# Heads dealt over both row halves, shifted products ahead of the scores, one maximum a round: an attention and expert kernel on one core

## What is computed

```
q, k, v    = split(layernorm(x) @ Wqkv + bqkv)          # 16 heads of 8
_, ka, va  = split(ctx @ Wqkv_aux + bqkv_aux)
p  = softmax(q k^T / sqrt(8));  pa = softmax(q ka^T / sqrt(8))
att = (1 - sigmoid(g)) * (p @ v) + sigmoid(g) * (pa @ va)
x  = x + tanh(g_xattn) * (att @ Wo + bo)
x  = x + tanh(g_ffn) * moe(layernorm(x))                 # 64 experts, top 8 of 4 of 8 groups, and a shared one
```

## Time and profile before

| | |
|---|---|
| runs | 859.24, 859.26, 859.61 us; median 859.26 |
| the profiled execution | 859.58 us, of which 857.8 us span |
| granted TensorE clock | 0.985 in the mean; half speed from 15.9 to 39.8 us, full after |
| busy | TensorE 826.2 us (96%), its weight loads 646.0, VectorE 683.6 (80%), ScalarE 566.8 (66%), GpSimd 637.3 (74%) |
| attention loop | from 36.4 us to about 288 us, 32 batches |

### The profile page before, as it was taken

One profiled execution on the slowest core, in us unless ns is written; L12 is line 12 of the kernel. 1 busy time (PEld: TensorE's weight loads), 2 busy tenths in 40 slices (PEclk: granted clock), 3 DMA queues, 4 the chain that ended last, 5 costly groups with the idle time before them and its releaser, 6 DMA issues.

```text
span 857.8 us, 20206 instructions
## 1 busy us (share of the span) xinstructions
PE 826.2 (96%) x6733; PEld 646.0 (75%) x6733; DVE 683.6 (80%) x1648; ACT 566.8 (66%) x964; POOL 637.3 (74%) x602
## 2 busy tenths in 40 slices
PE   4899999999999999999999999999999999999997
PEld 3477777777766678888888888878888888888885
DVE  6789999999897769769678877867966977876665
ACT  4388888888878665575576576557557557655554
POOL 2668888888854378877787786777777788778785
PEclk8599999999999999999999999999999999999999
DMA  4677786776652167447456554654654755546562
GB/s 119 173 169 173 178 183 155 187 169 170 160 126 51 53 152 169 120 111 184 117 142 147 131 142 125 154 135 109 163 139 111 171 130 134 149 116 150 137 138 58
DMA packets 108036, 120.04 MB, mean 140 GB/s; under 512 B 28560, under 2 KB 70352, under 8 KB 106496
## 3 DMA queue, kind: packets, MB, share of 16 engines
q1 hardware_dynamic: 105056, 118.23, 57.5%
q10 hardware_dynamic: 2880, 0.59, 0.4%
HBM read 103.55 MB, written 14.71 MB: 138 GB/s over the span
## 4 chain that ended last, share of the span: by engine, by line
PE 87%; DVE 5%; DMA 3%; issue 2%; SPq 1%; ACT 1%; POOL 0%; DVEq 0%; POOLq 0%
PE bank L1999 20%; PE bank L2000 20%; PE bank L2001 20%; PE bank L1336 7%; PE bank L1323 5%; PE bank L1294 3%; PE bank L1276 2%; PE bank L1344 2%; PE bank L1260 1%; PE bank L1357 1%; DVE mx L989 1%; PE bank L1270 1%; DMA cwb<-wts_scratch 1%; DMA stack_q<-nmaxT 1%; PE bank L1976 1%
## 5 line engine op out<-in xcount | busy, mean ns | idle before, releaser
L1676 POOL TENSOR_TENSOR hid<-act,cwb 128x512 f32<-128x512 f32 x264 | 424.0, 1615 | 126.4 <-DVE act L1903 69.1
L1729 ACT ACTIVATE silu<-bank 128x512 f32<-128x512 f32 x256 | 152.9, 597 | 190.7 <-PE bank L2001 189.9
L1903 DVE TENSOR_TENSOR act<-silu,bank 128x512 f32<-128x512 f32 (+1 forms) x264 | 180.5, 684 | 119.5 <-ACT silu L1729 78.7
L1999 PE MATMUL bank<-xhi,weights_hi 128*128 128x512 f32 x520 | 206.6, 397 | 0.0
L1911 DVE TENSOR_TENSOR hlo<-hid,hhi 128x512 fp32r<-128x512 f32 x256 | 197.5, 772 | 8.5 <-ACT hhi L1735 8.3
L2001 PE MATMUL bank<-xlo,weights_hi 128*128 128x512 f32 x520 | 204.2, 393 | 0.0
L2000 PE MATMUL bank<-xhi,weights_lo 128*128 128x512 f32 x520 | 203.9, 392 | 0.0
L1735 ACT ACTIVATE hhi<-hid 128x512 fp32r<-128x512 f32 (+1 forms) x264 | 164.8, 625 | 15.7 <-POOL hid L1676 13.1
L989 DVE TENSOR_REDUCE mx<-bank 128x4 f32<-128x512 f32 x240 | 156.0, 683 | 16.6 <-PE bank L1294 14.8
L786 ACT ACTIVATE prob<-bank 128x1024 f32<-128x1024 f32 x128 | 131.2, 1025 | 48.6 <-PE bank L1323 46.5
L2001 PEld LDWEIGHTS bank<-xlo,weights_hi 128*128 128x128 f32 x520 | 97.6, 188 | 22.0
(11 more groups left out here) (238 smaller groups left out, 1022.1 us busy)
## 6 DMA issues: line engine op xcount, KB each, us to landing
cwb<-wts_scratch SPq DMA_DIRECT2D x174, 384.0 KB, 5.4
stack_k<-k_scratch SPq DMA_DIRECT2D x30, 256.0 KB, 4.3
k_scratch<-parts_k SPq DMA_DIRECT2D x15, 384.0 KB, 3.4
stack_q<-q_scratch SPq DMA_DIRECT2D x30, 128.0 KB, 2.9
stack_k<-k_scratch SPq DMA_DIRECT2D x30, 128.0 KB, 5.2
q_scratch<-parts_q SPq DMA_DIRECT2D x15, 192.0 KB, 2.7
xin<-in_x_dram SPq DMA_DIRECT2D x16, 128.0 KB, 3.0
cin<-in_ctx_dram SPq DMA_DIRECT2D x16, 128.0 KB, 3.1
```

The costliest lines, as they stand in the source:

```text
L1676: pool.tensor_tensor(h_buf[k][:], a_buf[k][:], cwb[slot][:, q % GP, :], ALU.mult).then_inc(h_ok, 1)
L1729: act.activation(s_buf[k % RS][:], g_bank[k % 2][:], ACT.Silu).then_inc(s_ok, 1)
L1903: nc.vector.tensor_tensor(a_buf[k % RS][at], s_buf[k % RS][at], u_bank[k % 3][at], ALU.mult).then_inc(a_ok, 1)
L1999: nc.tensor.matmul(bank, w[0], mh, start=first, stop=False)
```

## The change

Heads are dealt in turn over the two halves: head h goes to row `ROW_OF[h]`, which is half h % 2, place h // 2. For this the weights of Q and K and their biases are reordered so (4-level patterns in place of 3-level ones); V and the output keep their order. The biases come in as rows, ScalarE reorders them, TensorE turns them into columns by three products with a one, and ScalarE copies these to `bcol`. The scores of a unit are still of one half and one bank, but the two units of a round are of different halves (`S_ROW`). In a round all 8 shifted products come first, half 0 and half 1 in turn, each half in a bank of its own; then the 4 scores, also in turn. One maximum of 128x1024 covers both score banks. The scores of a round therefore wait for the maximum of the whole round before. Both halves of a stack are waited for ahead of round 0. `first_scores` changes likewise.

The diff, cut to its core:

```diff
-S_HEAD = (8, 10, 12, 14, 0, 2, 4, 6)
+S_ROW = (0, 8, 2, 10, 4, 12, 6, 14)
+ROW_OF = tuple(h % 2 * (H // 2) + h // 2 for h in range(H))
...
     def bias_loads(sp):
-        turned = lambda a: a.rearrange("(h d a) -> d h a", d=DH, a=1)
-        for i, b in enumerate((turned(v["bqkv"][0:P]), turned(v["bqkv"][P:2 * P]), turned(v["bqkv_aux"][P:2 * P]))):
-            sp.dma_start(bcol[:, i:i + 1], b, allow_slow_non_contiguous=True).then_inc(c_in, 16)
+        sp.dma_start(brow_in[:, 0:2 * P], one(v["bqkv"][0:2 * P])).then_inc(c_in, 16)
+        sp.dma_start(brow_in[:, 2 * P:3 * P], one(v["bqkv_aux"][P:2 * P])).then_inc(c_in, 16)
...
+        def by_row(to, w):
+            act.activation(to.rearrange("p (d f i) -> p d f i", d=DH, f=2),
+                           w.rearrange("p (i f d) -> p d f i", d=DH, f=2), ACT.Copy).then_inc(wqk_ok, 1)
...
+        act.wait_ge(c_in, 16 * 2)
+        for i in range(3):
+            act.activation(brow[:, i * P:(i + 1) * P].rearrange("a (d f i) -> a d f i", d=DH, f=2),
+                           brow_in[:, i * P:(i + 1) * P].rearrange("a (i f d) -> a d f i", d=DH, f=2),
+                           ACT.Copy).then_inc(b_row, 1)
...
         evac_t(0, 0)
+        act.wait_ge(b_mm, 1)
+        act.activation(bcol[:], st_bank[0][:, 0:3], ACT.Copy).then_inc(b_ev, 1)
         clear_stack_q(0).then_inc(stack_clear, 1)
         clear_stack_q(1).then_inc(stack_clear, 1)
-        act.wait_ge(c_in, 16 * 3)
+        act.wait_ge(b_ev, 1)
         copy_q(0)
...
-        def maxima(b, par, u):
-            wait(dve, s_mm, UNITS * b + u + 1)
-            if u == 0:
+        def maxima(b, r, banks=two_banks):
+            wait(dve, s_mm, UNITS * b + 2 * r + 2)
+            if r == 0:
                 wait(dve, nm_ok, b - 1)
...
+            h = S_ROW[2 * r]
+            nc.vector.tensor_reduce(mx[b % 2][:, :, h:h + 2].rearrange("p (f a) h -> p f h a", f=2),
+                                    banks[:].rearrange("p (f h a k) -> p f h a k", f=2, h=2, a=2),
                                     AXX, ALU.max).then_inc(mx_ok, 2)
...
-                    if two_more:
-                        maxima(b + 2, odd, u)
+                    if two_more and u % 2 == 0:
+                        maxima(b + 2, u // 2)
                     if u == (1 if late else 0) and one_more:
                         evac_nmax(b + 1)
...
-        def stack_there(b, u):
+        def stack_there(b):
             n, c, s = b // CH, b % CH, b // CH % NST
             if c == 0:
-                wait(pe, stk[S_HEAD[u] // HH][s], 64 * ((n - 1) // NST + 1 if s else n // NST))
-            if u == 0:
-                wait(pe, shift_zero, CH if n == NST else b - CH * NST + 1)
+                for half in (1, 0):
+                    wait(pe, stk[half][s], 64 * ((n - 1) // NST + 1 if s else n // NST))
+            wait(pe, shift_zero, CH if n == NST else b - CH * NST + 1)
...
-            a, h = u % 2, (u // 2) * HPU + j
+            a, h = u % 2, ROW_OF[(u // 2) * HPU + j]
...
-            ins = nc.tensor.matmul(st_bank[u % 2][:, j * P:(j + 1) * P], k_of(n)[at, h % HH, c, a, :],
+            at_p = (a * 2 + j // 2) * P
+            ins = nc.tensor.matmul(st_bank[j % 2][:, at_p:at_p + P], k_of(n)[at, h % HH, c, a, :],
                                    q_of(n)[at, h % HH, c, :], start=True, stop=True)
-            if j == HPU - 1:
+            if a == 1 and j >= 2:
                 ins.then_inc(st_mm, 1)
...
         transposes(0, 0)
+        turn_biases()
         pe.wait_ge(wqk_ok, 3)
...
-                    if two_more and r % 2 == 0:
-                        stack_there(b + 2, 2 * r)
-                    for u in (2 * r, 2 * r + 1):
-                        ahead = (b + 2, u) if two_more else None
-                        shifted(b, u, 0)
-                        if ahead:
-                            scores(*ahead, 0)
-                        shifted(b, u, 1)
-                        shifted(b, u, 2)
-                        if ahead:
-                            scores(*ahead, 1)
-                        shifted(b, u, 3)
+                    if two_more and r == 0:
+                        stack_there(b + 2)
+                    u0, u1 = 2 * r, 2 * r + 1
+                    for u in (u0, u1):
+                        for j in range(HPU):
+                            shifted(b, u, j)
+                    if two_more:
+                        for j in range(2):
+                            scores(b + 2, u0, j)
+                            scores(b + 2, u1, j)
```

More of the change, by code:

```diff
@@ L227, in attention @@
     prob = [m(f"prob{i}", [P, 2, HPU * P], F32) for i in range(RP)]
+    brow, brow_in = (prob[0][0:1, k, 0:3 * P] for k in range(2))
     mx = [m(f"mx{i}", [P, 4, HH], F32) for i in range(2)]
@@ L1192, in on_dve @@
         for r in range(ROUNDS):
-            first_maxima(0, r)
+            maxima(0, r, (wide, two_banks)[r % 2])
         minus_max(0, 0, 3)
@@ L1198, in on_dve @@
         for r in range(ROUNDS):
-            first_maxima(1, r)
+            maxima(1, r, (wide, two_banks)[r % 2])
             if r == 1:
@@ L1301, in first_scores @@
             wait(pe, mx_ok, 2 * (pair - 1))
-            for u in (2 * r, 2 * r + 1):
-                for j in range(2):
-                    h = S_HEAD[u] + j
-                    if j == 0 and u in (0, 4):
-                        wait(pe, stk0[h // HH][b], 64)
+            if r == 0:
+                for half in (1, 0):
+                    wait(pe, stk0[half][b], 64)
+            for j in range(2):
+                for u in (2 * r, 2 * r + 1):
+                    h = S_ROW[u] + j
                     at = slice(*SCORE_ROWS[h // HH])
@@ L1358, in out_proj, with turn_biases @@
             nc.tensor.matmul(o, attT[:, 1, :], wo[:, 1, :], start=False, stop=True).then_inc(wo_mm, 1)
+        def turn_biases():
+            pe.wait_ge(b_row, 3)
+            pe.wait_ge(kones_ok, 4)
+            for i in range(3):
+                ins = nc.tensor.matmul(st_bank[0][:, i:i + 1], brow[:, i * P:(i + 1) * P], ones[0:1, 0:1],
+                                       start=True, stop=True)
+            ins.then_inc(b_mm, 1)
         def turn_max(b):
```

26 lines of the change are left out of this document (8 added, 18 removed).

## The result

| | before | after |
|---|---|---|
| median of the runs | 859.26 us (858.38 to 859.90, 5 runs) | 872.80 us (870.98 to 872.95, 5 runs) |
| the profiled execution | 859.58 us, span 857.8 | 870.98 us, span 869.2 |
| first batch of the loop starts | 36.43 us | 38.74 us |
| a pair of batches that no DMA delays | 15.59 us | 16.43 us |

A forecast was written before the change was run, and what follows sets the result against it. TensorE's own work was taken to bound five rounds of eight, the exponential loop three. 859.58 + 10.1 + 2.0 + 1.0 - 1.4 - 1.0 = 870.3 us, median 870.0; own range 865 to 875, stated 862 to 878.

The forecast's parts named there:

- What bounds the kernel: Attention stage: of eight rounds a pair, five are TensorE's own work, three are closed by shifted products, exponential, shifted products.
- the three waits: TensorE's waits for the exponential in three rounds of a pair: 0.1 us each over the gap, 0.3 a pair, would go.
- Part 1: Shifted products first over both halves: exponential starts at about +0.47 us, 0.22 earlier; TensorE's work stays, three waits go.
- Part 2: One maximum a round: 1.29 us becomes 1.21 on VectorE, starting at +0.64; the single buffer by itself costs nothing.
- The rival "faster": If nmaxT's DMA issue holds back nothing, the three waits go: 855.0 us, up to 859; chance 0.11.
- Part 3: Round 0: nmaxT's copy behind the whole maximum delays DMA issue, copy of Q and exponential; +0.78 us a pair, +10.1 total.
- There is a copy of Q in 13 odd batches: Loop: the count of batches that pay the delay behind nmaxT's DMA; of 16, the last three chunks have none; +10.1 us.
- Part 4: Both stack halves awaited ahead of round 0: stage start +2.0 us (0.8 to 3), late loads in the loop +1.0.
- The term of the loop: Six late stack loads, 4.1 us together, mostly forgiven by longer pairs: 0.5 left, +1.0 us taken, bounds 0 and 5.
- Part 5: Ends of the stage: -1.4 us in the last two batches, -1.0 in the three before; bias loads nothing.
- slower by the single buffer: Rival: scores wait for the maximum in most rounds; +5, 875 us; chance 0.07.
- The biases: Bias loads as rows, copies and small products lie beside other work: nothing, bounds 0 and +0.5 us.

The follow-up runs named there:

- e9_mended: Changed kernel with nmaxT's DMA issued in round 1, the maximum's semaphore stepping by 1, and first stores ahead of first loads: 862.19 us, 1.0032 of before.
- e1_ship_later: Changed kernel with only the issue of nmaxT's DMA moved, behind the copy of Q and round 1's exponential: 863.9 us, 1.0047 of before.
- e7_inc_one: Changed kernel with the joined maximum adding 1 to its semaphore instead of 2, waits on it counting rounds: 870.67 us, 1.0130 of before.
- e11_two_ship: Changed kernel with two maxima of 128x512 a round again and nmaxT's DMA issued in round 1 of every batch: 863.68 us, 1.0050 of before.
- e3_wide_on_before: Kernel before with only the joined 128x1024 maximum over both score banks a round: 873.40 us, 1.0155 of before.
- e5_copy_behind: Kernel before with only round 0's copy to nmaxT moved, behind both half maxima instead of between them: 866.49 us, 1.0072 of before.
- e4_both_halves: Kernel before with only the waits for both halves of a stack put ahead of round 0, first scores included: 863.13 us, 1.0043 of before.
- e6_bias_rows: Kernel before with only the new bias loads (two rows, three ScalarE copies, three products, one copy out): 860.91 us, 1.0010 of before.
- e10_wait_behind: Changed kernel, nmaxT's DMA in round 1, semaphore step 1, old store order, stack wait moved behind round 0's shifted products: 861.42 us, 1.0022 of before.
- e8_start_order: Kernel before with SP issuing the second chunk's first stores ahead of the first chunk's second-batch loads: 859.54 us, 0.9996 of before.

## Why the prediction came out right, step by step

**What bounds the kernel** held: rounds closed by TensorE's own work or by the loop shifted products, exponential, shifted products. With the hold gone e9_mended takes 0.24 us off a pair, near the 0.3 that the prediction gave to the three waits.

**Part 1** was right in its offsets: exponentials start at +0.47 (113.24 less 112.77), and the even round 3 gave the 0.09. The other two stood ahead of round 2 of each batch, where the holds of part 3 now stand; in e1_ship_later both of these rounds take 1.71 us (before 1.88 and 1.76).

**Part 2** gave 1220 ns for the joined maximum against 1214 expected. It said +0.64 for its start; it is +0.75 (+0.76 for 115.78 less 115.02). Of this miss of 0.11, e7_inc_one shows 0.07 to be the separate wait that comes with a step of 2. The rival "faster" failed: VectorE's work fell by 9.3 us and the time rose. It isn't empty, 0.19 us a pair with the hold gone and a step of 1 (e9_mended against e11_two_ship). The Trainium skill (Perfetto Trace Analysis, Optimizing Scalar/DVE Operations) says that grouping can raise throughput where the engine is saturated; VectorE had 1.3 us free in a pair, and this case's runs show a loss.

**Part 3**, the deciding step, against the trace of the odd batch:

| | said | measured |
|---|---|---|
| maximum of round 0 starts | +1.10 | +1.23 |
| copy of nmaxT over | +2.44 | +2.53 |
| copy of Q starts | +3.22 | +3.32 |
| exponential starts | +3.66 | +3.70 |
| round 2 starts | +4.76 | +4.77 |
| price in the odd batch | +0.80 | +0.78 |
| price in the even batch | +0.07 | +0.15 |
| a pair | +0.78 | +0.84 |

The even batch's term was half its size: its exponential starts at +2.95 (108.00 less 105.05), not +2.84, so there the whole 0.1 by which the maximum starts late reaches the exponential. The first pair pays only 0.2 of the 0.78. The prediction also let nmaxT's landing keep the slack it had. From the issue in an odd batch that is so (6.1 us, before 6.2); from the issue in an even one 5.5 us are left of 6.0, and no wait came of it.

The cause is shown step by step: e3_wide_on_before shows that the joined maximum brings the hold, e5_copy_behind that the copy's place does it without any other operation, and e1_ship_later that the DMA's wait in ScalarE's order carries it to TensorE. "There is a copy of Q in 13 odd batches" was too narrow a condition: in the even batch 26 the conversion of weights (line 818) stands behind the issue and waits 0.92 us for it just so.

**Part 4**: the start was right, +2.3 for +2.0, and e4_both_halves gives +2.8 for it alone; the traces of the kernels that start so scatter from 38.24 to 39.28 us. The term of the loop, +1.0, was wrong in sign. The longer pairs forgave all late half stacks, and also the 0.8 us of longer pairs that before had. The price exists, as e4_both_halves and e9_mended show, where a pair is 15.6 us or less.

**Part 5** was mis-sized: -2.4 said, -0.35 measured. In the last two batches five rounds gained 0.08 to 0.19 us, 0.8 together, and not seven 0.2; one, round 1 of the last batch, took 0.38 more, and the trace names no releaser for its idle time. In the batches 26 to 29 it is +0.25, not -1.0. Two rounds cost 0.5 each, and the others give back 0.7. One is round 1 of batch 26, with the hold named under part 3. The other is round 1 of batch 27: with the extra statistics on VectorE, TensorE's scores wait there for the maximum, which is the mechanism of the rival "slower by the single buffer", confined to the end of the stage. Its row in after:

```profile
263.51 0.39 PE L1297 MATMUL bank<-stack_k,stack_q 48*128 48x256 bf16 x4 [0.79 <-DVE mx L1000]
```

**The sum**: 10.7 us said for the profiled execution, 11.4 measured, from start +2.3 (+2.0), loop +9.45 (+11.1), ends -0.35 (-2.4). The misses of the loop, -1.65, and of the ends, +2.05, nearly cancel; that is luck, and the sum is better than its terms. The median, 870.0 said and 872.80 measured, misses by 2.8: 0.7 are these terms, and 2.1 are that the median of after lies 1.8 above its profiled execution and not 0.3 below it, which no trace explains. **The biases** started the stage 0.7 us later by themselves in e6_bias_rows, outside the bound of 0.5, and nothing of that is seen behind the later wait.

Not shown: a version faster than the kernel before. The best of the changed kernels stays 0.2% to 0.3% above it. Loads of the stacks issued earlier by SP were not tried in the loop, and they are what e9_mended's pairs of 15.35 would need.

## What to carry to other kernels

When two operations are joined, ask who stood between them and who waits in order behind that one: here a copy of 0.2 us, then a DMA issued by ScalarE, then the exponential on which TensorE waits. The saving is read from the operation's row, the price from the timeline of the engine that issues the DMA. And a shorter loop must find its transfers earlier: two edits took a pair from 16.43 to 15.35 us, and transfers that cost the kernel before 0.8 us in twelve pairs then cost 3.5, which took back nearly all that the shorter pairs had won.

## What the runs showed of the hardware

- The maximum that stepped its semaphore by 2 carried no wait; a separate one stood ahead, and the maximum started 0.065 us behind it. With a step of 1 the wait was part of the maximum (98 such instructions fewer in e7_inc_one, 0.14 us less in a pair). A met wait of TensorE ahead of round 2 cost 0.09 us (e4_both_halves), and one between shifted products and scores 0.08 (e10_wait_behind).
- A DMA's issue on ScalarE that stands behind an exponential in the program runs beside it (129.03 and 129.04 in e1_ship_later). One that stands ahead holds all that follows, for its wait and for its own 0.65 us (115.34 to 115.99, the copy of Q at 116.09 in after).
- Float32 products with one row of contraction, 128 weight columns and one moving column took two passes each, of 0.24 us (six in 1.44 us for three products, e6_bias_rows).
- The landing of nmaxT, a transfer of 16 KB, was waited for until 5.3 to 7.7 us after its issue (172.64 to 180.30 in e8_start_order is the longest), and such waits came and went between executions of the same loop.
